# GpSimd waits for the sums of the pair two behind, not four, in a two-layer graph network

## The reference, cut to what matters

```
layer 0: msgs = x_t[src] * e_t            # x_t: an MLP of the nodes; e_t: an MLP of 32 edge attributes
         out  = x + segment_sum(msgs, dst)
         x    = layernorm(x + layernorm(out) * gamma + beta)
layer 1: xw[r] = x @ rel_w[r]             # 8 relations; a table of 8 * 12500 rows
         msgs = xw[edge_type, src] * edge_weight
         x    = layernorm(x + relu(segment_sum(msgs, dst) + bias))
```

## Time and profile before

| what | value |
|---|---|
| median of three runs | 4873.86 us |
| the profiled execution | 4852.9 us, of which the span is 4851.1 us |
| GpSimd busy | 2998.0 us (62%) |
| TensorE busy | 1993.1 us (41%) |
| VectorE busy | 1488.5 us (31%) |
| ScalarE busy | 303.5 us (6%) |
| TensorE's granted clock | 0.632 of full |

### The profile page before, as it was taken

The page is one execution under the profiler, slowest core; times in us unless marked ns, Lnnn a source line. Parts: engine busy times, 40 slices in busy tenths (PEclk is TensorE's granted clock), DMA queues, the critical chain, the costliest instruction groups (busy, mean ns, idle before and its releaser), DMA issues.

```text
span 4851.1 us, 32143 instructions
## 1 busy us (share of the span) xinstructions
PE 1993.1 (41%) x6900; PEld 1435.4 (30%) x6901; DVE 1488.5 (31%) x3786; ACT 303.5 (6%) x628; POOL 2998.0 (62%) x3223
## 2 busy tenths in 40 slices
PE   6545545454555554555554222232222232222322
PEld 5333333333333333333332121121221221222222
DVE  4323333333333333333333222222222222223223
ACT  3000000000101111011111000000000000000000
POOL 6566656655655565555553666766666666666665
PEclk8776666666676676667776555555555555555555
DMA  4111111111111111121111111111111111111111
GB/s 103 31 33 34 34 32 44 33 43 43 44 43 43 42 44 35 43 52 43 49 33 51 24 24 24 25 24 24 25 25 24 25 26 27 25 24 27 27 27 25
DMA packets 199836, 169.83 MB, mean 35 GB/s; under 512 B 83053, under 2 KB 135425, under 8 KB 199523
## 3 DMA queue, kind: packets, MB, share of 16 engines
q0 software_dynamic: 100032, 102.60, 11.9%
q1 hardware_dynamic: 99202, 64.51, 4.5%
q10 hardware_dynamic: 288, 0.07, 0.0%
HBM read 134.87 MB, written 32.10 MB: 34 GB/s over the span
## 4 chain that ended last, share of the span: by engine, by line
another core or an unknown queue 34%; issue 29%; PE 11%; DVE 9%; POOL 8%; DVEq 7%; ACT 2%; ACTq 1%; DMA 0%; SPq 0%; POOLq 0%
POOL rows L641 4%; POOL acc L641 4%; PE ps_agg L1472 3%; DVE acc L1082 2%; PE ps_z L1448 2%; PE ps_o L1464 2%; DVE work L1071 2%; DVE work L1162 2%; ACT low L702 1%; DVEq L1096 1%; DVEq L1082 1%; DVEq L1086 1%; DVEq L1148 1%; DVEq L1061 1%
## 5 line engine op out<-in xcount | busy, mean ns | idle before, releaser
L1472 PE MATMUL ps_agg<-work 128*128 128x192 f32 x2348 | 733.8, 457 | 1711.7 <-DVE work L1162 941.6
L1472 PEld LDWEIGHTS ps_agg<-work 128*128 128x128 f32 x2348 | 551.8, 265 | 1924.1 <-DVE work L1162 987.6
L641 POOL DMA_INDIRECT rows<-rel_table,row_ix x800 | 755.9, 945 | 449.2 <-issue 234.3
L641 POOL DMA_INDIRECT acc<-node_table,acc x763 | 720.6, 944 | 490.9 <-PE ps_agg L1472 235.3
L641 POOL DMA_INDIRECT rows<-node_table,acc x760 | 718.1, 945 | 489.6 <-issue 214.3
L641 POOL DMA_INDIRECT acc<-rel_table,row_ix x763 | 719.7, 943 | 337.3 <-issue 226.3
L1129 DVE SCALAR_TENSOR_TENSOR hid<-ps_z,b1e_c,low 128x512 f32<-128x512 f32 x196 | 147.1, 751 | 1327.1 <-ACT low L702 1014.3
L1082 DVE TENSOR_TENSOR acc<-acc,ps_agg 64x96 f32 x1174 | 288.5, 246 | 824.5 <-remote 644.9
L1071 DVE TENSOR_TENSOR work<-ps_x,rel 128x768 f32<-128x768 f32 x392 | 372.0, 949 | 39.8 <-issue 38.7
L1448 PE MATMUL ps_z<-attrT,W1e_d 128*128 128x256 f32 (+1 forms) x784 | 377.8, 616 | 7.5 <-issue 7.5
L1464 PE MATMUL ps_o<-W2e_d,hid 128*128 128x128 f32 x1564 | 345.9, 390 | 0.0
(11 more groups left out here) (167 smaller groups left out, 1235.9 us busy)
## 6 DMA issues: line engine op xcount, KB each, us to landing
attr<-in_edge_attr_dram SPq DMA_DIRECT2D x39, 640.0 KB
rel_table<-acc SPq DMA_DIRECT2D x19, 1280.0 KB
rows<-rel_table,row_ix POOLq DMA_INDIRECT x800
acc<-node_table,acc POOLq DMA_INDIRECT x763
acc<-rel_table,row_ix POOLq DMA_INDIRECT x763
rows<-node_table,acc POOLq DMA_INDIRECT x760
node_table<-work SPq DMA_DIRECT2D x24, 128.0 KB, 2.0
out_dram<-x_sb SPq DMA_DIRECT2D x19, 160.0 KB
```

Of the source, the lines that this page charges most:

```text
L641: nc.gpsimd.indirect_dma_start(ring[t % RING][0:n, j, :], None, table, bass.IndirectOffsetOnAxis(ap=lists[0:n, t, j : j + 1], axis=0),).th ...
L1472: last = nc.tensor.matmul(bank[:, 0 : 2 * W], data[:, 2 * jj : 2 * jj + 2, :], hot[:, 2 * jj : 2 * jj + 2, :], start=(jj == 0), stop=(jj = ...
```

## The change

One number: the distance, in pairs, of GpSimd's wait in front of each pair's first gather. No instruction is added, removed or moved on any engine. The wait now also stands in front of the pairs 2 and 3 of each layer, and everywhere it asks for a semaphore value that is higher by two.

```
@@ -440,7 +440,7 @@
         ZERO_FIRST, CAST_FIRST, PARTS_AT, REL_W_FIRST = 2, 27, 12, 17
         SPANS_AT = (32, 33, 35, 36, 38, 39, 41, 42, 44, 45)
         NORM_AFTER = 1
-        SUMS_BEHIND = 4
+        SUMS_BEHIND = 2
         TURN_AFTER, FIRST_AFTER, SECOND_AFTER = 2, 3, 4
```

## The result

The changed kernel takes 4899.28 us (median of 6 runs, 4888.28 to 4905.54), the kernel before beside it 4873.68 us (6 runs, 4872.34 to 4875.28): a ratio of 1.0051, 95% interval 1.0039 to 1.0063, or +25.6 us. The forecast was 4915 us. The profiled execution of the change took 4903.17 us with a span of 4901.3 us, which is 50.2 us over the span of before. Only half of that is in the medians: the profiled execution of before is not one of the six runs and lies 21 us under their median, that of after lies 4 us over its own.

What follows compares the result with a forecast made beforehand. The prediction took GpSimd's back-to-back gathers, broken by pauses waiting for TensorE's sums, as the bound. Terms +5 + 0 - 14 + 50 = +41 us on 4852.9, plus 21.0 us to the median, gave 4915 us, range 4825 to 5040.

Steps and rivals of the forecast that it cites:

- (a): Start of layer 0: GpSimd stops two pairs sooner, which may free the stalled setup; +5 us, bounds 0 and +20.
- (b): Layer 0's body: the typical pause costs the same with either limit; 0 us, bounds -50 and +100.
- (c): End of layer 0: only two pairs left after the last wait, not four; -14 us, bounds -18 and 0.
- (d): Layer 1's body: slack falls from 26.6 to 6.6 us; +50 us, bounds -62 and +172; waits rise to 70 or more.
- the 33 absorbed stalls: Layer 1: at least 84 - 51 VectorE stalls hidden by today's slack, each to exceed the new slack by 1.5 us.
- the first rival: Stalls shorten the sooner GpSimd stops, so series of pauses merge; -71 us, 4803 us; chance 0.30.
- Single pauses of over 12 us: Sign in layer 1's GpSimd waits that the forecast is wrong and stalls keep their length.
- the third rival: VectorE's stalls don't depend on GpSimd, so the rest beyond 6.6 us becomes pause; +163 us, 5037 us; chance 0.11.
- The sum of +41 us: Whole kernel: +5 + 0 - 14 + 50 us, added to the profiled execution's 4852.9 us, giving 4893.9 us.
- Stops cure stalls: Both layers: every stall is shorter the sooner GpSimd stops, merging series of pauses; -71 us, 4803 us; chance 0.30.
- Only pauses end stalls: Number and length of pauses stay as today, only layer 0's start and end count; -9 us, 4865 us; chance 0.14.
- Stalls keep their length: VectorE's stalls ignore GpSimd's stopping; each absorbed one costs at least a pause of today; +163 us, 5037 us; chance 0.11.

## Why the prediction was right, point by point

**The sign and the mechanism.** The forecast was slower, by lost slack in layer 1. It holds: layer 1's pauses rose by 43 us of wait and its length by 58 us, four or six behind absorb more than two, and without stalls layer 1 loses nothing. Without stalls the change is slower too (+34 us), but by layer 0, for a reason that the forecast didn't have.

**(a) Start of layer 0, +5 us.** L1037 came at 97.97, foreseen near 98; pair 2's wait ended at 117.50, foreseen near 124. Pair 4's first gather is at 140.46 and was at 139.47: +1.0 us, within its bounds of 0 and +20. That stopping earlier frees the setup is right. Without stalls there is nothing to free, and the full pause of 14.5 us is paid.

**(b) Body of layer 0, 0 us, and (c) its end, -14 us.** Measured +18.5 and -19.5 us, together -1. They belong together and should have been one term: where the other engines set layer 0's length, a tighter limit only moves waiting from the end into the body. As one term the sum of -14 was 13 us too good for this profile and lay inside the 0 to -19 us of all kernels with this limit and stalls. The bound of -18 for (c) was 1.5 us too near. Its row was misread as well: the additions at 2601.50 are still the pair before the last one's, and the last pair's own stand at 2611.66, 46.7 us after its first gather and not 36.5. After the change the two lags are 15.5 us (the sign said about 20) and 26.0 us; the saving is 21 us by either.

**(d) Body of layer 1, +50 us.** Measured +58.0 us in this profile and +37.5 us in another kernel with the same limit there. The direction was right, but that the size fits is in good part luck. I let the 33 absorbed stalls each stick out by 1.5 us. In fact the stalls behind them shortened to 7.6 us at most, as the first rival said, and only 13 waits came on top (64 in all, where the sign asked for 70 or more). What the first rival missed, and I with it, is the crawl: a slow VectorE that a pause of 1 to 3 us doesn't end. The waits that the profile puts down to TensorE's sums rose from 8 of 25.9 us to 26 of 153.4 us, and the longest, of up to 12.7 us, lie in crawls; those without a known releaser fell from 43 of 238.3 us to 38 of 153.8 us. "Single pauses of over 12 us" was my sign for the third rival; one of 12.7 us appeared, but with VectorE's stalls short, so the sign was badly chosen.

**The end of layer 1, 0 us.** Measured -7.7 us; the last pairs lag less. Not foreseen, though layer 0's end had the same reason.

**From the sum to the median.** The sum of +41 us stands against +50.3 in the profiles and +25.6 in the medians. I added the 21.0 us by which the profile of before lay under its median; the changed kernel's profile lies 3.9 us over its own. Which part of the kernel took those 21 us in the other runs can't be told, as they have no profile here.

**The rivals.** "Stops cure stalls" was right on the stalls and wrong on their worth: cured stalls had been absorbed. "Only pauses end stalls" fails on the number of pauses, 64 and not 51. "Stalls keep their length" is out by 678.4 us that became 89.4 us. The rule in the Trainium skill, SBUF — State Buffer, "Who interferes with whom", which stood behind it, is about ports; what seems to tie the engines to the gathers here shows in the semaphores' updates.

## What to carry to other kernels

A limit on how far one engine may run ahead is worth the lateness that it has to cover: find the longest lateness of the engines it waits for, and set the limit above it; a looser one bought nothing here (six as four, without stalls and with stalls of 15 us put in, where it cost time at the end), and below it a lateness costs at most its excess (1.7 to 4.7 us for a stall that exceeded the slack by 8.6). Look for that lateness at the start and at work that is inserted now and then as well as in the steady part, since there the steady slack says nothing. And measure a kernel in more than one session before tuning it to its stalls, which may not be the kernel's own: here a sixth of the time was the session's, and the change costs 0.5% with stalls and 0.8% without, each for another reason.

## What the runs showed of the hardware

- The same kernel took 4039 us and 4851 us on one chip in two sessions, and within a session its runs lay within 0.6% of each other. In the two profiles of the kernel before that have stalls, GpSimd pauses before the same 51 pairs of layer 1.
- In the sessions with stalls only between a seventh and a quarter of the updates of semaphores from the gathers are in the trace (3584 to some 6160 of some 25,000), VectorE adds sums up to 25 us after TensorE has finished them (over at 3887.41, added at 3912.76 in the earlier trace rows), and its sequencer's small instructions take some 0.70 us each in stretches of up to 55 us; without stalls those in layer 1 take under 0.10 us, loads of registers aside.
- Beside VectorE's addition of 128x1280 numbers a gather takes 1.22 us and not 0.94 (the row at 2956.67 above), and the first one that starts beside it mostly longer, up to 2.24 us. The Trainium skill, SBUF — State Buffer, "Who interferes with whom", gives VectorE and GpSimd one shared pair of ports, and the trace agrees that the additions slow the gathers.
